# Division of the attention values in channel rows through DRAM for eleven octets, and later second norms, in a windowed attention block on one core

## What is computed

```python
y = roll(layernorm(x, g1, b1), (-2, -2))           # then windows of 128 tokens
q, k, v = split(xw @ qkv_w + qkv_b)                # 4 heads of 8
attn = softmax(q * SCALE @ k.T + bias + mask)      # 128 x 128 per head and window
o = (attn @ v) @ proj_w + proj_b
x = x + roll(unwindow(o), (2, 2))
z = layernorm(x, g2, b2)
return x + gelu(z @ fc1_w + fc1_b) @ fc2_w + fc2_b
```

## Time and profile before

| | us |
|---|---|
| median of 3 runs | 214.7 (212.72, 214.7, 215.17) |
| profiled execution | 213.55 |
| its span | 211.7 |

### The profile page before, as it was taken

One profiled execution on the slowest core, in us unless ns is written; L12 is line 12 of the kernel. 1 busy time (PEld: TensorE's weight loads), 2 busy tenths in 40 slices (PEclk: granted clock), 3 DMA queues, 4 the chain that ended last, 5 costly groups with the idle time before them and its releaser, 6 DMA issues.

```text
span 211.7 us, 10978 instructions
## 1 busy us (share of the span) xinstructions
PE 190.5 (90%) x4768; PEld 115.9 (55%) x4768; DVE 157.1 (74%) x221; ACT 146.6 (69%) x217; POOL 134.1 (63%) x148
## 2 busy tenths in 40 slices
PE   0789869798989999999999999999999998979884
PEld 0754534456556657656665676576567654443212
DVE  3895956675768878876987888687766977657874
ACT  7555378645868588768867895877557656588883
POOL 7786399671246995999499869844762291702730
PEclk9999979999999999999999999999999999999999
DMA  6924538656433741554365236414620000000324
GB/s 187 273 65 143 172 125 246 165 174 191 137 119 105 217 141 60 176 155 132 107 182 161 81 112 177 127 62 152 207 58 5 8 5 6 3 0 3 150 99 152
DMA packets 24296, 25.61 MB, mean 121 GB/s; under 512 B 3556, under 2 KB 21732, under 8 KB 24164
## 3 DMA queue, kind: packets, MB, share of 16 engines
q1 hardware_dynamic: 23496, 24.16, 37.3%
q10 hardware_dynamic: 752, 0.74, 1.3%
HBM read 16.24 MB, written 8.39 MB: 116 GB/s over the span
## 4 chain that ended last, share of the span: by engine, by line
PE 53%; POOL 13%; issue 13%; ACT 7%; SPq 5%; DVE 4%; DMA 3%; POOLq 0%; DVEq 0%; ACTq 0%
PE pav L992 10%; PE ps L957 9%; PE ps L972 7%; POOL rstd L403 4%; SPq L213 4%; PE ps L943 4%; PE ps L919 4%; PE ps L1010 3%; POOL parts L421 3%; PE pq L1094 3%; PE pq L880 2%; PE pq L1100 2%; ACT prob L765 2%; DMA X<-x_tok 2%; ACT q_rows L770 2%
## 5 line engine op out<-in xcount | busy, mean ns | idle before, releaser
L560 DVE TENSOR_REDUCE m_parts<-ps 128x8 f32<-128x1024 f32 x64 | 78.1, 1222 | 31.7 <-PE ps L943 31.4
L765 ACT ACTIVATE prob<-ps 128x1024 f32<-128x1024 f32 x64 | 65.5, 1024 | 34.9 <-PE ps L972 33.6
L403 POOL TENSOR_TENSOR rstd<-var,neghalf 128x16 f32<-128x16 f32 x16 | 47.4, 2963 | 8.2 <-DVE var L525 7.3
L992 PE MATMUL pav<-prob,va 128*32 128x128 f32 x1024 | 42.2, 278 | 0.2 <-issue 0.2
L957 PE MATMUL ps<-rel_j,id_b 96*32 96x512 bf16 x512 | 40.2, 380 | 2.2 <-DVE m_parts L560 0.9
L972 PEld LDWEIGHTS ps<-q_rows,k_rows 64*64 64x64 bf16 x1024 | 16.9, 106 | 27.0 <-issue 22.4
L992 PEld LDWEIGHTS pav<-prob,va 128*32 128x32 f32 x1024 | 24.8, 109 | 9.5 <-ACT prob L765 4.6
L972 PE MATMUL ps<-q_rows,k_rows 64*64 64x128 bf16 x1024 | 27.6, 224 | 1.8 <-DMA q_rows<-m_rows 1.6
L943 PEld LDWEIGHTS ps<-k_rows,q_rows 64*64 64x64 bf16 x1024 | 22.7, 108 | 6.5 <-issue 0.6
L943 PE MATMUL ps<-k_rows,q_rows 64*64 64x128 bf16 x1024 | 25.6, 217 | 0.0
L919 PE MATMUL ps<-rel_i,ident_b 64*64 64x512 bf16 x256 | 25.3, 383 | 0.0
(11 more groups left out here) (128 smaller groups left out, 309.4 us busy)
## 6 DMA issues: line engine op xcount, KB each, us to landing
slots<-parts SPq DMA_DIRECT2D x21, 256.0 KB, 3.0
q_rows<-slots SPq DMA_DIRECT2D x42, 128.0 KB
k_rows<-slots SPq DMA_DIRECT2D x40, 128.0 KB
X<-x_tok SPq DMA_DIRECT2D x8, 256.0 KB, 4.0
y_tok<-res SPq DMA_DIRECT2D x7, 256.0 KB, 2.0
q_rows<-m_rows SPq DMA_DIRECT2D x32, 8.0 KB
bias_parts<-rel_parts SPq DMA_DIRECT2D x3, 128.0 KB
slots<-parts SPq DMA_DIRECT2D x3, 128.0 KB, 3.5
```

Of the source, the lines that this page charges most:

```text
L403: pool.tensor_tensor(rstd[:, i, :], var[:, i, :], neghalf[:], ALU.pow).then_inc(rstd_done[i], 1)
L560: dve.tensor_reduce(dst, first_home(j)[:].rearrange("p (a u n) -> p a u n", u=2, n=TOK), AX.X, ALU.max, negate=True).then_inc(max_done, 1)
L765: act.activation(prob[:, j % NPROB, :], ps2[:], ACT.Exp).then_inc(exp_done, 1)
L992: mm = pe.matmul(pav[32 * h:32 * (h + 1), 128 * (j % 4):128 * (j % 4 + 1)], va[:, b % 2, at:at + 32], prob[:, j % NPROB, src:src + 128], s ...
```

## The change

For octets 0 to 10 (BY_ROWS = 11) the two transposes are left out. The values are divided where they stand, in rows of channels. The sums, 8 rows of 512 in oT, are sent to 128 x 32 (sums_col), inverted, sent to DRAM, and read back with each row spread over 16 partitions (rec_wide, 128 x 512). VectorE multiplies oT by rec_wide (scaled), and TensorE projects straight from it with a new weight layout wpr into Q0. The steps of an octet are now: p = 4q+5 copy oT, then behind the exponential the issue of sums_col; 4q+7 invert_sums and behind the exponential the issue to DRAM; 4q+9 behind the exponential the issue of rec_wide; 4q+11 scale_values; 4q+12 project_rows and add_attention. oT has two halves now. All three DMAs are issued by ScalarE. Octets 11 to 15 go as before, except that project_out is always the form with two matmuls of 128 rows. The projection now stands behind transpose_first in TensorE's order. The second norms of images 0 to 3 begin 8 pairs later, that of image 4 four pairs later, image 5 as before.

```diff
+BY_ROWS = 11
+        def second_begin(m):
+            return PPI * (m + 2) + 4 if m < 4 else PPI * (m + 2) if m == 4 else PPI * (m + 1) + 4
+        def second_due(p, steps):
+            return [m for m in range(B - 2) if p - second_begin(m) == steps]
+        def octet_at(p, steps, rows):
+            q, r = divmod(p - steps, 4)
+            return r == 0 and (0 <= q < BY_ROWS if rows else BY_ROWS <= q < OCTETS)
...
+            def invert_sums(q):
+                dve.wait_ge(d_sums[q % 2], 16 * (q // 2 + 1))
+                after(dve, d_recs[q % 2], 16 * (q // 2))
+                dve.reciprocal(rec_col[:, q % 2, :], sums_col[:, q % 2, :]).then_inc(rcol_done, 1)
+            def scale_values(q):
+                dve.wait_ge(d_wide[q % 2], 16 * (q // 2 + 1))
+                after(dve, proj_done, q)
+                dve.tensor_tensor(scaled[:], oT[:, q % 2, :], rec_wide[:, q % 2, :], ALU.mult).then_inc(scaled_done, 1)
...
+                if octet_at(p, 12, True):
+                    add_attention((p - 12) // 4)
+                if octet_at(p, 7, True):
+                    invert_sums((p - 7) // 4)
+                if octet_at(p, 11, True):
+                    scale_values((p - 11) // 4)
...
                 if 0 <= p < PAIRS:
                     exponential(p)
                 if late_rows(p):
                     max_rows((p + 2) // 2)
+                if octet_at(p, 7, True):
+                    q = (p - 7) // 4
+                    act.wait_ge(rcol_done, q + 1)
+                    after(act, d_wide[q % 2], 16 * (q // 2))
+                    act.dma_start(sum_scratch[q % 2], rec_col[:, q % 2, :]).then_inc(d_recs[q % 2], 16)
+                if octet_at(p, 9, True):
+                    q = (p - 9) // 4
+                    act.wait_ge(d_recs[q % 2], 16 * (q // 2 + 1))
+                    after(act, scaled_done, q - 1)
+                    act.dma_start(rec_wide[:, q % 2, :],
+                                  sum_scratch[q % 2].unsqueeze(1).to_broadcast([8, 16, 512])).then_inc(d_wide[q % 2], 16)
+                if octet_at(p, 5, True):
+                    q = (p - 5) // 4
+                    act.wait_ge(oT_done, q + 1)
+                    after(act, rcol_done, q - 1)
+                    act.dma_start(sums_col[:, q % 2, :], oT[HD:128:16, q % 2, :]).then_inc(d_sums[q % 2], 16)
...
+            def project_rows(q):
+                pe.wait_ge(scaled_done, q + 1)
+                b = (4 * q + 12) // PPI
+                if q % 2 == 1:
                     pe.wait_ge(va_done, min(b + 1, B))
                 elif b + 2 < B:
                     pe.wait_ge(rest_done, 2 * (b + 2) + 2)
+                for j in range(4):
+                    for c in range(4):
+                        at = 128 * j + 32 * c
+                        mm = pe.matmul(Q0[32 * c:32 * (c + 1), 64 * j:64 * (j + 1)], scaled[:, at:at + 32], P("wpr"),
+                                       start=True, stop=True)
+                mm.then_inc(proj_done, 1)
...
-                if s == 4 and 0 <= b - 1 < B - 2:
-                    mean_of(second_norm(b - 1))
-                    center(second_norm(b - 1), b - 1)
+                for m in second_due(p, 0):
+                    mean_of(second_norm(m))
+                    center(second_norm(m), m)
```

More of the change, by code:

```diff
@@ L485, in _ @@
                     scale(first_norm(b + 3))
-                if s == 7 and 0 <= b - 1 < B:
-                    if b - 1 < B - 2:
-                        variance_of(second_norm(b - 1))
-                    power(second_norm(b - 1))
+                for m in second_due(p, 3):
+                    variance_of(second_norm(m))
+                    power(second_norm(m))
+                if p == PAIRS - 1:
+                    power(second_norm(B - 2))
                 if p == PAIRS:
@@ L850, in _ @@
                     square(first_norm(b + 3))
-                if s == 5 and 0 <= b - 1 < B - 2:
-                    square(second_norm(b - 1))
+                for m in second_due(p, 1):
+                    square(second_norm(m))
             for m in range(B):
@@ L1115, in project_out @@
                     pe.wait_ge(rest_done, 2 * (b + 2) + 2)
-                for t in range(2):
-                    for c in range(2):
-                        at = 128 * t + 64 * c
-                        for gp in range(2):
-                            rows = slice(64 * gp, 64 * (gp + 1))
-                            mm = pe.matmul(po[64 * c:64 * (c + 1), 2 * gp:2 * gp + 2, C * t:C * (t + 1)],
-                                           onT[rows, at:at + 64], P("wp")[rows, rows], start=True, stop=True)
+                for j in range(4):
[4 more added lines that the diff above has]
+                mm.then_inc(proj_done, 1)
+            def project_out(q):
+                pe.wait_ge(onT_done, q - BY_ROWS + 1)
+                for t in range(2):
+                    mm = pe.matmul(pch[:, 128 * t:128 * (t + 1)], onT[:, 128 * t:128 * (t + 1)], P("wp"),
+                                   start=True, stop=True)
                 mm.then_inc(proj_done, 1)
@@ L1258, in _pack @@
                 wp[at:at + HD, C * g:C * (g + 1)] = p["proj_w"][HD * h:HD * (h + 1)]
+    wpr = part("wpr")
+    for h in range(HEADS):
+        for wi in range(2):
+            at = 32 * h + 16 * wi
+            wpr[at:at + HD, C * wi:C * (wi + 1)] = p["proj_w"][HD * h:HD * (h + 1)]
     return a
```

104 lines of the change are left out of this document (53 added, 51 removed).

## The result

The change makes the kernel slower, and by more than the forecast's range allowed: 235.86 us median of 4 runs (230.94 to 239.75), against 214.94 us for the kernel before in the same sitting (212.72 to 215.79). The ratio is 1.0908, 95% interval 1.0847 to 1.0969. Medians here are of all executions, while a ratio leaves out slow ones (here 237.62 and 239.75 us, over 1.5% above the shortest and at a lower clock), so I give sizes by the ratios too. The forecast was 218.5 us with a range up to 222.5. The profiled execution is the longest of the four (span 237.9); a part of its excess over the shortest one (span 229.1) goes with the clock, so I read mechanisms from it and not sizes.

The account below looks back on a forecast made before the run. It took the pulse of exponentials, with a 2.09 us floor, and GpSimd's norm chain as bounds; -0.4, +0.5, +4.1, +0.3 and +0.7 made +5.2 us on 213.55, 218.7, stated as 218.5; range 210.5 to 222.5.

Parts of the forecast that it names:

- The wide transfer just fits: Reciprocals' spread, 256 KB, 4.0 us from issue to landing against two periods of at least 4.2 us less the issue; counted 0.
- the other end: VectorE's waits for the new transfers: 1 us per octet, about 8 us in all, instead of the 0 taken.
- rival C: Transfers landing over 4.5 us after issue make VectorE and bias_s1 late: +4 on the sum, 222.5 us; chance 0.10.
- ScalarE's issues: Two DMA issues behind the exponential of place 1 put 0.3 to 0.7 us on the path; period into place 2 is 2.75.
- The floor: Next scores wait until the exponential has read the one PSUM tile ps2, so a pair's period cannot go under 2.09 us.
- The projection: TensorE, places 0 and 4: 16 matmuls at 0.70 us; at place 0 nothing hides it behind the transposition.
- the +4.1 us: Pairs 20 to 43, three images: 1.1 us each from GpSimd's delay and the projection, plus 0.35 - 0.07 at places 2 and 3.
- the sign that I had asked for: TensorE idle before the transposition at place 0, released by GpSimd's yn, some 0.5 us or more in three images.
- Late norms of images 3 to 5: Later second norms of these images cost 0, since VectorE, ScalarE and GpSimd have room there.
- VectorE at place 3: Added reciprocal (0.35 at most) and 128x512 product (0.69) delay the norm's sum, and so yn, by 0.5 us.
- The rule of 8 engines: Skill page's rule: 8 rows on one side give all three transfers 8 engines, against 16 for the X load, so later landing.
- matmul busy time should have fallen by 5 to 8 us: TensorE over the whole kernel: busy matmul time lower by 5 to 8 us while the span grows.

Follow-up runs that it names:

- experiment 4: Changed kernel without the wide transfer, product by constant 1: 222.17 us; or with it cut to 32 columns instead of 512, all issues and waits kept: 225.81 us.
- experiment 2: Changed kernel without its three transfers, values not divided by their sums: 222.37 us with constants set at the start, 222.53 us without that setting.
- experiment 5: Changed kernel with the sums issued by SyncE at the head of places 1 and 5: 234.53 us; or by ScalarE ahead of the wide transfer: 234.08 us.
- experiment 8: Changed kernel with BY_ROWS = 0; early norms: 217.10 us with projection behind the transposition, 215.15 ahead; late norms, projection ahead: 216.27 us.
- the kernel with the narrow transfer: Changed kernel with the spread of the reciprocals carrying 32 columns instead of 512, every transfer still issued and awaited: 225.81 us, ratio 1.0506.
- SyncE's kernel: Changed kernel with the sums issued by SyncE at the head of places 1 and 5, ahead of its gathers: 234.53 us, ratio 1.0936.

## Why the prediction was wrong

The sign was right, and the direction of the argument (no matmul time is to be won, since the pulse has a floor) held. The size was off by 17 us at the median (16 by the ratio). Point by point:

- **The transfers, the step that failed.** "The wide transfer just fits ... I take 0, with 1 us per octet, about 8 us in all, as the other end." The runs show the other end and more: 7 to 10 us for the wide transfer's bytes alone (experiment 4), 11 to 13 us for everything of the transfers (experiment 2), that is 1.0 to 1.2 us per octet. It was rival C, at 0.10, and it too was priced low (+4). The wide transfer itself landed about when the forecast said (4.1 us in the median, against 4.0 for X in the earlier trace rows). What failed is the other half of the step. For the sums behind it the only row was the small send's 2.15 us; these 16 KB took 4.4 us in the median and up to 6.8, and VectorE stood 13.4 us for them. And "just fits" left no room: with the sums ahead of it the wide transfer landed at 4.8 us in the median and VectorE stood 10.5 us for that (experiment 5). The range left out an end that the forecast itself had named: 218.5 + 8 = 226.5 lay outside it. Even that end would not have covered 235.86.
- **Who else pays.** The forecast asked only whether VectorE would have its operand in time. 4 to 6 us are there when it does not wait for sums or wide rows. The landing of m_rows (a wait of 4.8 us there, 2.2 without transfers) and ScalarE's issues and waits may be parts of it; how they divide was not tried.
- **The clock was not in the sum.** A stall of 3 us of TensorE is followed by matmuls at 1.2 GHz (1.08 us for 0.65). By the busy time above it is some 4 us of the profiled execution; in the shortest one, with its clock of 0.993, it must be less.
- **ScalarE's issues: right.** Two issues behind an exponential, forecast 0.3 to 0.7 us on the path and a period into place 2 of 2.75. The rows:

```profile
131.92 1.02 ACT L797 ACTIVATE prob<-ps 128x1024 f32<-128x1024 f32 x1 [0.15 <-PE ps L1024]
131.98 0.60 ACTq L883 DMA_DIRECT2D rec_wide<-value_sums  x1
132.68 0.61 ACTq L889 DMA_DIRECT2D sums_col<-oT  x1
133.39 0.63 ACT L780 ACTIVATE parts<-rest 128x512 bf16<-128x512 f32 x1 [0.45 <-issue]
...
134.66 1.00 ACT L797 ACTIVATE prob<-ps 128x1024 f32<-128x1024 f32 x1
135.71 0.62 PE L1009 MATMUL ps<-rel_j,id_b 96*32 96x512 bf16 x8 [0.73 <-ACT prob L797]
...
136.72 1.02 ACT L797 ACTIVATE prob<-ps 128x1024 f32<-128x1024 f32 x1 [1.07 <-PE ps L1024]
```

  The first issue starts 0.06 us after the exponential's start, the next activation 1.47 us after it instead of 0.92, and the period is 134.66 - 131.92 = 2.74. It is 2.74 in four images of this trace in a row.
- **The floor: right.** The next period, into place 3, is 136.72 - 134.66 = 2.06 with bias_s2 waiting for the exponential, against 2.09 in the earlier trace rows.
- **The projection: right in size, likely right in place.** 0.65 us for its 16 matmuls (I used 0.70). In the kernels without octets in rows its place behind the transposition costs 1.2 to 2.6 us (experiment 8), under the +4.1 us that I had for it with GpSimd's and ScalarE's parts. That TensorE waits for yn shows in the rows at 120.94 (0.31, changed kernel) and 131.87 (0.38, experiment 8). But the sign that I had asked for, 0.5 us or more in three images, did not come: the waits of the changed kernel for GpSimd's yn are 0.7 us in two times.
- **Late norms of images 3 to 5: "room there, 0".** Likely wrong, by 0.7 to 1.7 us. Room by busy share, but not at the moment when middle_max is due.
- **VectorE at place 3: half right.** I counted the delay for the sums of the norm, not for the remainder behind which the new projection itself waits: 4.0 us in five waits. The product I took at 0.69: it is 0.63 alone, and mostly longer where a 128x512 product of GpSimd runs beside it, as in these rows of the kernel with the narrow transfer (GpSimd's product yn runs from 134.47 to 135.52):

```profile
134.41 0.34 DVE L583 RECIPROCAL rec_col<-sums_col 128x32 f32<-128x32 f32 x1
134.66 1.41 DVE L588 TENSOR_TENSOR scaled<-oT,rec_wide 128x512 f32<-128x512 f32 x1
```

- **The rule of 8 engines.** The page "DMA: Bandwidth & Descriptors" of the Trainium skill, section "Why a DMA increments its semaphore by 16 and not by 1", spoke against the change by way of the 8 rows on one side. By the same section each engine that takes part in a transfer adds one to its semaphore at its end, so completions count engines. The trace bears the rule out for two of the three: the queue of ScalarE has 5328 packets, and 3832 with the wide transfer left out (experiment 4), so 136 for each of eleven, which are its 128 rows and 8 completions. By the packets of 4 bytes and the semaphores' updates the sums have 8 too; the send of the reciprocals has 16, where the forecast had 8. The line of the kernel without the wide transfer stands below. What the 8 engines cost is not shown. The wide transfer landed at 4.1 us in the median, hardly later than X, and with the same 8 engines and a sixteenth of the bytes the waits nearly went. A wide transfer of the same bytes over 16 engines was not tried, and stays a rival for a part of the cost.

```profile
q10 hardware_dynamic: 3832, 1.10, 2.3%
```

The way from one kernel to the other in medians: 214.4, +0.8 for the projection in its new form (not in the forecast; ratio 1.0074), +2.0 for its place, +1.7 for the late norms, +3.7 for the octets' work without transfers, +3.3 for small transfers with all issues and waits (225.81 - 222.53), +10.0 for the wide transfer's bytes: 235.9. By the ratios the same six steps are 1.6, 1.2, 1.2, 4.8, 2.1 and 8.6 us, 19.5 together. The forecast had the first four at 4 us where they are 8 to 9, and the last two at 0 where they are 11 to 13.

What stays open: matmul busy time should have fallen by 5 to 8 us and fell by 3.4 at full clock (190.5 to 187.1); the ends of matmuls are modelled, and I have no run that separates this. Nor was it tried to spread the wide transfer over 16 engines, or to start the wide transfer two periods earlier, which would need the reciprocals sooner.

## What to carry to other kernels

Before a transfer is put on the path of a tuned kernel, read the DMA share in the very stretch in which it will run, and who else has a landing due there; its landing time in a quieter stretch is a lower bound, and beside 256 KB a small transfer or the large one itself came late here, whichever was issued second. Swapping two issues moved the wait, fewer bytes removed most of it: a sixteenth of the bytes gave back 7 to 10 of the 21 us. And where a cost's other end is 8 us and nothing in the rows excludes it, it belongs inside the range, the more so since a stall of TensorE can also bring a stretch at half clock.

## What the hardware showed that I had not expected

- A 16 KB transfer took 6.8 us from issue to use while the 16 engines were 83 to 85% busy, mostly with others' packets; with nothing large ahead of it in its queue it took 1.9 us in the median (experiment 5), and a send of 8 KB in the kernel before 2.15 us.
- Behind the stall of TensorE of 2.94 us the matmuls from 124.51 to 130.4 ran at 1.2 GHz, and the same profile has three more such stretches, at stalls of 4.4, 1.7 and 2.6 us. Not every stall is followed by one: SyncE's kernel of experiment 5 has stalls of 1.66 and 2.09 us before 166 and 172.7 us, and a clock of 1.00 from 160 to 180. The clock differed from run to run of the same kernel: 0.993 at 230.94 us, 0.964 at 239.75 us.
- A DMA issue on ScalarE started 0.06 us after an exponential's start and overlapped it, but the next activation still came 0.55 us later with two between; an issue with 16 KB to DRAM took 0.32 us of the queue instead of 0.61.
- A 128x512 product of VectorE took 0.63 us alone and up to 1.41 us with GpSimd at work on the same size of tiles. It is not always VectorE that pays: in the kernel without the wide transfer (experiment 4) the product at 115.45 kept its 0.63 us, and GpSimd's yn, begun at 115.36, took 1.62 us instead of 1.05.
